# Slot attention: two norms folded into weights, the deviations applied in the turning product, and a new written-out order

## The reference

```
def _ln(x, g, b): mu = mean(x); var = mean((x - mu)**2); return (x - mu) * rsqrt(var + 1e-5) * g + b
x_in = _ln(ctx, lnkv_g, lnkv_b);  k = x_in @ wk + bk;  v = x_in @ wv + bv
slots = q_mu + exp(q_logsig) * _layernorm(x)
for _ in range(3):
    prev = slots
    q = _ln(slots, lnq_g, lnq_b) @ wq + bq
    attn = softmax(k @ q.T / scale, over the slots) + 1e-8, divided by its sum over the context
    slots = attn.T @ v @ wu + bu + prev
    h = _ln(slots, lnm_g, lnm_b) @ w1 + b1
    slots = gelu(h) @ w2 + b2 + slots
    slots = _ln(slots + cond, lnp_g, lnp_b)
x = x + slots
```

## Time and profile before

| | |
|---|---|
| profiled execution's own time | 913.3 us |
| its span | 911.5 us |
| median of the timed runs | 911.91 us |
| mean granted TensorE clock | 0.912 |
| busy: TensorE, VectorE, ScalarE, GpSimd | 86%, 62%, 58%, 40% |
| slot stage, from its first measurement to the last send | 648.9 to 845 us |

### The profile page before, as it was taken

One profiled execution on the slowest core, in us unless ns is written; L12 is line 12 of the kernel. 1 busy time (PEld: TensorE's weight loads), 2 busy tenths in 40 slices (PEclk: granted clock), 3 DMA queues, 4 the chain that ended last, 5 costly groups with the idle time before them and its releaser, 6 DMA issues.

```text
span 911.5 us, 18113 instructions
## 1 busy us (share of the span) xinstructions
PE 781.2 (86%) x5705; PEld 645.1 (71%) x5705; DVE 568.4 (62%) x1974; ACT 529.7 (58%) x1144; POOL 360.8 (40%) x561
## 2 busy tenths in 40 slices
PE   6988799999999999989988778999968786861693
PEld 5766678878888788777876547999646565651693
DVE  1667777787776667776767653333658787874012
ACT  3665566667666677656756422333359898841462
POOL 1233444343443333332346562665413232226363
PEclk9999899999999999999989979999757979785797
DMA  8324405340701520301140044886600000001574
GB/s 263 111 66 148 143 1 168 113 178 25 267 1 30 177 57 5 99 1 33 57 161 26 25 145 135 246 248 191 215 0 1 1 1 1 1 1 39 166 200 137
DMA packets 82057, 88.54 MB, mean 97 GB/s; under 512 B 6156, under 2 KB 69852, under 8 KB 81324
## 3 DMA queue, kind: packets, MB, share of 16 engines
q1 hardware_dynamic: 78475, 80.19, 29.1%
q0 software_dynamic: 3488, 7.20, 2.2%
HBM read 69.03 MB, written 35.17 MB: 114 GB/s over the span
## 4 chain that ended last, share of the span: by engine, by line
PE 58%; DVE 20%; issue 8%; ACT 6%; POOL 5%; DMA 1%; DVEq 0%; SPq 0%; POOLq 0%; ACTq 0%
PE bank L706 6%; PE bank L1017 6%; PE bank L700 6%; DVE sb_smax L1531 4%; PE bank L733 4%; PE bank L773 3%; DVE sb_row_sum L1540 3%; PE bank L742 3%; PE bank L1025 3%; PE bank L838 3%; PE bank L758 2%; PE bank L1126 2%; PE bank L1134 2%; PE bank L715 2%; DVE sb_st_all L1857 2%
## 5 line engine op out<-in xcount | busy, mean ns | idle before, releaser
L2035 POOL TENSOR_TENSOR sb_expd<-sb_expd,sb_rden 128x512 f32<-128x512 f32 (+1 forms) x128 | 112.4, 879 | 243.5 <-DVE sb_rden L1544 243.3
L1531 DVE TENSOR_REDUCE sb_smax<-bank 128x4 f32<-128x512 f32 (+1 forms) x128 | 74.0, 578 | 66.7 <-PE bank L733 35.6
L2127 POOL TENSOR_TENSOR sb_rstd_all<-sb_rsq_all,sb_halves 128x4 f32<-128x4 f32 x44 | 45.2, 1028 | 131.6 <-DVE sb_rsq_all L1864 131.6
L1254 ACT ACTIVATE sb_expd<-sb_shifted 128x512 f32<-128x512 f32 (+1 forms) x128 | 69.7, 544 | 43.4 <-DVE sb_shifted L1534 42.4
L1540 DVE TENSOR_REDUCE sb_row_sum<-sb_expd 128x4 f32<-128x512 f32 (+1 forms) x128 | 73.0, 570 | 8.4 <-ACT sb_expd L1254 8.4
L1534 DVE TENSOR_TENSOR sb_shifted<-bank,sb_smax 128x512 f32<-128x512 f32 (+1 forms) x128 | 74.9, 585 | 4.4
L700 PE MATMUL bank<-sb_h1T,sb_watt 128*128 128x128 f32 x512 | 71.3, 291 | 4.2 <-ACT sb_h1T L1153 2.3
L700 PEld LDWEIGHTS bank<-sb_h1T,sb_watt 128*128 128x128 f32 x512 | 65.5, 204 | 6.8 <-DMA sb_watt<-att_w 2.7
L1017 PE MATMUL bank<-sb_blk_xT,sb_up_w 128*128 128x128 f32 x456 | 57.1, 275 | 0.0
L1017 PEld LDWEIGHTS bank<-sb_blk_xT,sb_up_w 128*128 128x128 f32 x456 | 54.0, 192 | 0.0
L1824 DVE TENSOR_TENSOR sb_hid<-bank,sb_hid 128x384 f32<-128x384 f32 x38 | 21.2, 558 | 51.1 <-ACT sb_hid L1302 51.1
(11 more groups left out here) (270 smaller groups left out, 2006.9 us busy)
## 6 DMA issues: line engine op xcount, KB each, us to landing
sb_up_w<-gate_up SPq DMA_DIRECT2D x38, 384.0 KB
sb_v<-v_all SPq DMA_DIRECT2D x16, 576.0 KB, 6.6
rows_b<-pad_b SPq DMA_DIRECT2D x7, 1105.0 KB, 9.8
rows_a<-pad_a SPq DMA_DIRECT2D x7, 975.0 KB, 8.0
sb_up_w<-w1b SPq DMA_DIRECT2D x23, 256.0 KB
v_all<-sb_moe_w SPq DMA_DIRECT2D x14, 308.0 KB
sb_blk_x<-rows_a SPq DMA_DIRECT2D x38, 65.0 KB, 3.3
sb_picked<-back_a SPq DMA_DIRECT2D x4, 512.0 KB, 5.5
```

The source lines that it names most:

```text
L1254: act.activation(exp_of(i, s, j), shifted[:, u % 2, :, 0:n], ACT.Exp, scale=DH ** -0.5).then_inc(exp_done, 1)
L1531: dve.tensor_reduce(smax[:, u % 2, :], s_in, X, ALU.max).then_inc(max_done, 1)
L2035: pool.tensor_tensor(e, e, rden[:, u % 2, :].unsqueeze(2).broadcast_to([P, QH, n]), ALU.mult).then_inc(norm_done, 1)
```

## The change

The gain of the query norm and of the hidden layer's norm goes into their weights, and so does the subtraction of the mean: with centring = I - 1/128, the weights are formed once as wq_fold = (gain * wq, centred) and w1_fold = centring @ (gain * w1), and the norms' biases go through the weights into bq_fold and b1_fold. `norm_q` (for it < 3), `norm_m`, `shift_q` (for it < 3) and `shift_m` are gone. GpSimd gets a step `diag_q` or `diag_m` behind each root: one operation that multiplies the unit matrix by the four tiles' inverse deviations and writes four diagonal matrices into zs. The turning product is now S (the slots) times the diagonal matrix, a real product instead of a transpose; `scale_q` and `scale_m` are plain copies. The products with the unit matrix in `layer2` become a step of their own, `base`, with two products of 512 columns in place of eight of 128. The preparation gets three VectorE operations, four products and four ScalarE operations more. The table of the order is written anew, with numbers in one common time scale.

```diff
 SLOT_STEPS = {
-    (-1,): {
-        "add": (-7.7126, -8.1139, -3.1663, -2.2100),
...
+    "measure_q": (0, ((6.7, 16.3, 20.5, 34.4,), (44.7, 51.7, 62.1, 74.6,), (84.9, 91.9, 102.2, 114.7,), (125.0, 132.7, 142.5, 158.2,),)),
+    "root_q": (0, ((8.4, 17.9, 22.1, 36.1,), (46.4, 53.4, 63.7, 76.2,), (86.5, 93.5, 103.8, 116.3,), (127.4, 135.1, 144.9, 162.0,),)),
+    "diag_q": (0, ((9.4, 19.0, 23.2, 37.2,), (47.5, 54.4, 64.8, 77.3,), (87.6, 94.6, 104.9, 117.4,),)),
+    "turn_q": (0, ((10.5, 20.0, 24.2, 38.9,), (49.3, 55.5, 65.8, 79.1,), (89.5, 95.6, 105.9, 119.2,), (143.1, 140.1, 148.1, 165.2,),)),
...
+    "max": (0, ((13.9, 25.1, 29.4, 46.3,), (53.3, 63.6, 70.8, 86.4,), (93.4, 103.7, 110.9, 127.3,),)),
...
+    "measure_m": (0, ((23.6, 36.2, 41.9, 56.1,), (66.3, 76.3, 82.1, 96.2,), (106.4, 116.5, 122.2, 138.4,),)),
+    "turn_m": (0, ((27.3, 40.2, 45.7, 59.8,), (70.0, 80.3, 85.8, 99.9,), (110.1, 120.4, 125.9, 142.2,),)),
+    "base": (0, ((29.4, 42.8, 47.6, 63.1,), (72.3, 83.0, 87.7, 103.3,), (112.4, 123.1, 127.8, 145.2,),)),
+    "layer1": (0, ((32.1, 42.1, 50.3, 62.4,), (74.1, 82.2, 90.4, 102.5,), (114.2, 122.3, 129.6, 144.1,),)),
+    "layer2": (0, ((35.4, 44.6, 56.4, 64.9,), (76.4, 84.8, 96.5, 105.1,), (116.5, 124.9, 133.3, 147.0,),)),
+    "gate": (3, ((144.9, 143.6, 149.5, 166.6,),)),
+    "choose": (3, ((150.3, 167.4,),)),
+    "rank": (3, ((152.6, 169.7,),)),
+    "place": (3, ((153.7, 170.3,),)),
+    "send": (3, ((157.0, 163.1, 168.1, 173.6,),)),
...
 pe:
+            t = slot_bank()
+            pe.wait_ge(fold_ready, 1)
+            pe.matmul(t[:, 0:P], wq_gain[:, :], centring[:, :], start=True, stop=True)
+            pe.matmul(t[:, P:2 * P], centring[:, :], w1_gain[:, :], start=True, stop=True)
...
+            def turn_group(it, g, k):
+                pe.wait_ge(diag_ready[k], nth("diag_" + k, it, g))
+                for n, b in enumerate(tiles(g)):
+                    mm = pe.matmul(quads(bank[2 * g])[:, n, :], S[:, b, :], zs[:, b, :], start=True, stop=True)
...
+                if step == "base":
+                    pe.wait_ge(mid_ready, nth("updated", it, g))
+                    pe.wait_ge(zT_ready["m"], nth("scale_m", it, g))
+                    pe.matmul(bank[2 * g][:, :], eye[:, :], flat(S, g), start=True, stop=False)
+                    pe.matmul(bank[2 * g][:, :], eye[:, :], flat(cb2, g), start=False, stop=False)
                 if step == "layer2":
-                    pe.wait_ge(mid_ready, nth("updated", it, g))
                     pe.wait_ge(hid_ready, nth("gelu", it, g))
                     for n, b in enumerate(tiles(g)):
-                        pe.matmul(quads(bank[2 * g])[:, n, :], eye[:, :], S[:, b, :], start=True, stop=False)
-                        pe.matmul(quads(bank[2 * g])[:, n, :], eye[:, :], cb2[:, b, :], start=False, stop=False)
-                        mm = pe.matmul(quads(bank[2 * g])[:, n, :], hid[:, b, :], w2s, start=False, stop=True)
+                        mm = pe.matmul(quads(bank[2 * g])[:, n, :], hid[:, b, :], w2s, start=False, stop=(n == 3))
 act:
+                if step in ("scale_q", "scale_m"):
+                    k = step[-1]
+                    act.wait_ge(zT_done[k], nth("turn_" + k, it, g))
+                    act.activation(group_of(zsT, g), bank[2 * g][:, :], ACT.Copy).then_inc(zT_ready[k], 1)
...
 pool:
+            def diagonal(k, g, count):
+                pool.wait_ge(root_ready[k], count)
+                pool.tensor_tensor(group(zs, g), eye[:, :].unsqueeze(1).broadcast_to([P, 4, P]),
+                                   rstd_all[:, 4 * g:4 * g + 4].unsqueeze(2).broadcast_to([P, 4, P]), ALU.mult).then_inc(diag_ready[k], 1)
```

More of the change, by code:

```diff
@@ L111 @@
 SLOT_STEPS = {
-    (-1,): {
-        "add": (-7.7126, -8.1139, -3.1663, -2.2100),
[L114 to L155, removed]
+    "add": (-1, ((0.0, 1.3, 9.8, 26.3,),)),
@@ L161, in slot_steps @@
 def slot_steps(*names):
-    found = [(4 * (it + 1) + g + phase, name, it, g) for its, kinds in SLOT_STEPS.items() for name in names if name in kinds
-             for it in its for g, phase in zip(ROUTING_AT.get(name, range(4)), kinds[name])]
-    return [step[1:] for step in sorted(found)]
+    found = [(time, names.index(name), name, it, g) for name in names for it, times in enumerate(SLOT_STEPS[name][1], SLOT_STEPS[name][0])
+             for g, time in zip(ROUTING_AT.get(name, range(4)), times)]
+    return [step[2:] for step in sorted(found)]
 def streams(i):
@@ L500, in program @@
         passed = {name: {step[1:]: n + 1 for n, step in enumerate(slot_steps(name))}
-                  for kinds in SLOT_STEPS.values() for name in kinds}
+                  for name in SLOT_STEPS}
         def nth(name, it, g):
@@ L1064, in _ @@
                 mm.then_inc(pre_slot_full, 1)
-            pe.wait_ge(pre_slot_done, 5 * G + 1)
-            def turn_group(it, g, k, src=zs):
-                pe.wait_ge(z_normed[k], nth("norm_" + k, it, g))
-                for n in range(4):
-                    mm = pe.transpose(quads(bank[2 * g])[:, n, :], src[:, 4 * g + n, 0:D], eye[:, :])
-                mm.then_inc(zT_done[k], 1)
-            for step, it, g in slot_steps("turn_q", "logits", "update", "turn_m", "layer1", "layer2", "gate", "rank"):
-                if step == "turn_q":
-                    turn_group(it, g, "q", zs if it < SLOT_ITERS else sent[0])
+            pe.wait_ge(pre_slot_done, 5 * G + 2)
+            def turn_group(it, g, k):
+                pe.wait_ge(diag_ready[k], nth("diag_" + k, it, g))
+                for n, b in enumerate(tiles(g)):
+                    mm = pe.matmul(quads(bank[2 * g])[:, n, :], S[:, b, :], zs[:, b, :], start=True, stop=True)
+                mm.then_inc(zT_done[k], 1)
+            for step, it, g in slot_steps("turn_q", "logits", "update", "turn_m", "base", "layer1", "layer2", "gate", "rank"):
+                if step == "turn_q" and it < SLOT_ITERS:
+                    turn_group(it, g, "q")
+                if step == "turn_q" and it == SLOT_ITERS:
+                    pe.wait_ge(z_normed["q"], nth("norm_q", it, g))
+                    for n, b in enumerate(tiles(g)):
+                        mm = pe.transpose(quads(bank[2 * g])[:, n, :], sent[0][:, b, 0:D], eye[:, :])
+                    mm.then_inc(zT_done["q"], 1)
                 if step == "logits":
@@ L1874, in _ @@
             dve.wait_ge(exp_out["a"], len(PARTS["a"]) + 1)
-            for step, it, g in slot_steps("add", "measure_q", "shift_q", "max", "share_sum", "updated", "measure_m", "shift_m",
+            for step, it, g in slot_steps("add", "measure_q", "shift_q", "max", "share_sum", "updated", "measure_m",
                                           "measure_o", "centre", "slots", "gated", "choose", "place"):
@@ L1910, in _ @@
                     measured(g, S, "m")
-                if step == "shift_m":
-                    shifted_by(it, g, "m")
                 if step == "measure_o":
```

85 lines of the change are left out of this document (54 added, 31 removed).

## The result

The changed kernel took 922.96 us (median of 4 runs, 921.07 to 925.55) against 911.87 us (910.87 to 915.03): ratio 1.0118, 95% interval 1.0079 to 1.0156. A second measurement beside the experiments gave 1.0100 (1.0084 to 1.0117). A ratio is always to runs of the kernel before taken beside the kernel in question; their median was 911.9, 913.4 or 916.9 us, so that times of different sessions are not compared. The profiled execution has a span of 922.1 us, 10.6 more than before.

What follows compares the result with a forecast made beforehand. VectorE was taken to bound the iterations (40.8 of 44.0 us). First send at 800.3 + 28, plus 21.4 us of sends, put the last send 5.5 us later: 911.9 + 5.5 = 917.4 us, range 903.5 to 923.5.

Steps and rivals of the forecast that it cites:

- measure_m 3: VectorE's hidden-layer measurement of group 3 in iteration 2: predicted to start at 800.3 us, against 797.97 before.
- the hold-up: VectorE and GpSimd shutting each other out: named for slots against diagonals, up to 1 us per meeting, left out of the sum.
- First max: Start of the slot stage on VectorE: first maximum predicted at 674.0 us, against 673.41 before.
- Stall at the first updated: Start of the stage: VectorE waits 2.3 us for group 0's update on TensorE, until 684.4 us.
- Period: VectorE between like steps of successive iterations: 40 to 42 us, floor 39.5, against 44.0 before.
- Diagonals: 24 GpSimd operations of 128x512: 1.06 us each assumed, 25 to 31 us in all, GpSimd not binding.
- The end: From measure_m 3 to the first send: TensorE sparse and at half clock, 28 us taken, 20.4 at full clock.
- Sends: GpSimd's indirect DMAs at the stage's end: 21.4 us from first to last, against 19.07 before.
- What follows is untouched: Behind the last send: no change in time assumed, so the span grows only by the last send's 5.5 us.
- Rival 1: VectorE stays fed and TensorE's clock holds at the stage's end: 4.4 us faster, 907.5 us; chance 0.26.
- Rival 3: TensorE at half clock bounds the periods: 5 us more per period, 928 us; chance 0.06.
- Rival 2: Periods gain 2 x 2 to 3 us and the stage's end gives them back: 910 to 915 us; chance 0.24.

Runs made afterwards that it cites:

- e6: Changed kernel with each GpSimd diagonal writing 128x4 instead of 128x512 values, so the result is not computed; ratio to the kernel before 0.9925.
- e7: e3 with group 1's slots and measure_q ahead of the first max, and group 3's base ahead of the gate products; ratio to the kernel before 1.0000.
- e2: Changed kernel with the variance instruction written as a tensor_scalar with one tensor operand instead of two; ratio to the kernel before 1.0079.
- e3: Changed kernel with ten dummy products nobody reads filling TensorE's gaps at the stage's end; ratio to the kernel before 1.0003.
- e8: Kernel before, unchanged, profiled a second time; the first step_b product came 11.03 us after the last send, not 6.53.
- e1: Changed kernel's work in the order of the kernel before, each diagonal right behind its root; ratio to the kernel before 0.9980.
- e12: Kernel before with a GpSimd diagonal behind each of 24 roots, written to a buffer nobody reads; ratio to the kernel before 1.0118.

## Why the prediction was right, and where not

Forecast 917.4 in 903.5 to 923.5, slower: it came out at 922.96, slower, 0.5 us inside the edge of the range. That is partly luck: the interval of the ratio reaches beyond the edge. The forecast of the span was 5.1 us short (917.0 against 922.1): 3.85 at measure_m 3, -1.6 to the first send, 0.4 in the sends and 2.4 behind them. That it came out slower is partly luck as well. The sum left out the hold-up, and e6, the run nearest to a kernel without it, was 0.75% faster than before; since e6 also has shorter diagonals, it stays open what the forecast's own terms would have given alone. By its steps:

- **First max** 674.0: 673.34, but 671.34 in the second profile; the work ahead varies by more than this agreement. Stall at the first updated: 2.3 us by 684.4; 1.21 us, at 683.41, about half. A was 3.0 us longer than before. Moving the two steps from behind the max gave 3.3 us back (e7), and the smaller diagonal with the order kept 2.2 to 2.9 (e6), so these runs do not say which of the two the loss came from.
- **Period** 40 to 42 with a floor of 39.5: 41.25, against 44.0. e6's second period of 39.36 is the floor.
- **Diagonals** 1.06: 1.07 us in the mean. Right as a duration; what it costs VectorE was missing.
- **The step that failed** is the sentence "in the sum below it is left out". By the Trainium skill, "SBUF — State Buffer", section "Who interferes with whom", VectorE and GpSimd exclude each other when both need a shared port pair. The stretched rows agree in kind (0.16 us became up to 0.86, until the diagonal's end). That term measured 7.6 us of VectorE's time up to measure_m 3; the way there was 6.3 us shorter in e6. e6 needed 124.5 us from first max to measure_m 3, so the prediction's 122.8 + 2.3 + 1.2 = 126.3 comes near without the term. After it was 130.8, and measure_m 3 came at 804.15 instead of 800.3. I had also named the wrong victim: slots lost 56 x 0.028 = 1.6 us, the variance instructions 39 x 0.16 = 6.2.
- **The form with one operand.** By the Trainium skill, "SBUF — State Buffer", section "Who interferes with whom", `tensor_scalar` can enter a two-port mode and then contend too. e2 agrees (309 ns, against 162 undisturbed); its expectation had not weighed this.
- **The end** at half clock: right. The clock was 0.50 when the turning of group 3 ran; measure_o 3 came 16.96 us after measure_m 3 (18.8 predicted), the first send 26.4 (28). The clock did not come back within base and layer2, as the prediction took it to: they took 2.06, 1.91 and 1.71 us. e3 shows what the half clock costs: with the clock up behind the turning, 4.6 us return and the ratio goes to 1.0003. By e3 this end is what keeps the kernel from a tie. In e6 the clock came back sooner, which the prediction did not foresee.
- **Sends** 21.4 us: 21.78. The last send came 8.2 us later than before where 5.5 was forecast: +3.85 at measure_m 3, where the hold-up is the missing term, -1.6 by the end, +0.4 by the sends.
- **"What follows is untouched"** missed 2.4 us in the compared pair of profiles. e8 shows that the kernel before can have this distance too, so the sentence may stand for the code and fails for that one profile.
- **Rival 1** (the clock holds at the end) did not come of itself; e7 shows it with the clock at 0.98 from 800 to 812 us, and even then only a tie. **Rival 3** (half clock bounding the periods) did not come: their clock was 0.98 in 697 to 785 us against 0.84 before. Real products for transposes alone bring little of this: e1, with the old order, had 0.88. **Rival 2** had the gain in the periods right, 5.7 us for two, and was wrong that the end only gives it back.

## What to carry to other kernels

Before moving work to GpSimd beside a busy VectorE, count every small VectorE instruction that can fall beside it and price each meeting at up to the whole GpSimd instruction; e12 measured 11 us for 24 products that nobody read. Then test an order and a change of work apart: here the work, hold-up included, was worth -1.6 us and the order +9.8. Where TensorE is sparse ahead of a serial tail, look at the granted clock first: ten idle products took 4.6 us out of the stretch ahead of it.

## What was not expected of the hardware

- A GpSimd product of 128x512 (1.04 us) held a VectorE instruction of 0.16 us up to 0.86 us, until its own end. Held up were 128x4 instructions with two tensors in SBUF, a `tensor_scalar` with one, slots and the addition to x (1046 ns against 687 in e6). Not held up: batch norm statistics (279 to 285 ns in all these kernels) and aggregates (157), and max from PSUM (680).
- In that contention GpSimd lost little: its diagonals stayed at 1.04 us. The single ones of 1.32 and 1.47 us (at 687.71 and 790.75) each started 0.26 and 0.12 us behind an addition to x on VectorE: there VectorE was first, and it was GpSimd that took longer.
- SyncE's first issue of expert weights came 1.5 to 3.8 us behind the start of the last send in thirteen profiles, however early its tables were ready, and 2.3 us ahead of it in one, the first of the kernel before. The same code gave both; the cause is open.
